# Norm and turn of the tokens for two mixtures moved into the attention ahead of each

## The chip, the cores and the metric

The kernel runs on one core of one Trainium2 chip. The metric is the device time of one execution in microseconds (us). Engines are named as in the profile: PE is TensorE's matmul, PEld its weight load, DVE is VectorE, ACT is ScalarE, POOL is GpSimd, SP is SyncE.

## The reference

The program is four layers over 16 batches of 100 tokens with 256 features. Each layer adds a gated cross attention and then a gated mixture to x. What bears on the change, in short:

```
x = x + tanh(g_xattn[1]) * attention1(layernorm(x), ctx)        # 8 heads of 64
x = x + tanh(g_ffn[1])   * squared_mixture(layernorm(x))
x = x + tanh(g_xattn[2]) * attention2(layernorm(x), ctx)        # 4 heads of 64
x = x + tanh(g_ffn[2])   * linear_mixture(layernorm(x))

squared_mixture(x): shared = square(relu(x @ Ws1)) @ Ws2
                    weight = trunc(softmax(top 2 of x @ Wr))    # 8 experts
                    shared + sum_e weight_e * (square(relu(x @ W1_e)) @ W2_e)
linear_mixture(x):  weight = softmax(top 2 of x @ gate)         # 8 experts
                    sum_e weight_e * (x @ weight_e)
```

The context has 361 rows of 192 features. All of it is float32. A product of two float32 tiles stands in the trace as two records, a transpose as one.

## The kernel before, in words

The program has eight phases on one core: attention 0, a routed mixture, attention 1 (L=1), the squared mixture, attention 2 (L=2), the linear mixture, attention 3, the slot mixture. The order on each engine is the order in which the code is written; engines meet by semaphores. Two phases are parted by `end` and `begin`: each of PE, DVE, ACT and POOL raises `phase_ended` when it has drained, and each waits for all four. Attention 1 follows the routed mixture, and attention 3 the linear mixture, without such a meeting in full.

An attention goes over the batches one at a time (`pipelined`: batches 0, 1, 14 and 15 are written out, the others are a hardware loop of two). While batch t is attended, PE computes the projections of batch t+1 (`step`) and closes batch t-1 (`o_turn`, `project`). Heads come in pairs: four pairs in attention 1, two in attention 2. DVE takes the maxima of the scores (`maximum`, L1440), copies the turned probabilities out of PSUM (`probs_copy`, L1449), which PE needs for `weigh` (L2268), scales the output (`o_scale`, L1456 and L1462), which PE needs for `o_turn` (L2277), and adds the closed batch to X (`residual`, L1470, L1475, and the statistics L1483). `residual(t-1)` stands behind the maxima of heads 2 and 3 and ahead of `probs_copy` of heads 2 and 3.

A mixture of before starts by making its own input from X. `x_stats` (L1631, L1633) reduces the statistics of all 16 batches, POOL raises all 16 columns to the power -0.5 (L827), `pair_norm` (L1639) normalizes one batch, `pair_turn` on PE (L2473) turns two batches into a bank, and `pair_copy` on ACT (L1093) copies them to GXT, the turned tokens that every product of the mixture reads. In the squared mixture PE then computes the logits of all 13 tiles of 128 tokens (`tile_logits`, L2485), and only then the hidden products (`hidden`, L2502: four groups of 400 tokens, nine experts with the shared one) and the products back (`down`, L2518). DVE chooses the experts from the logits (L1648 to L1678) and adds the outputs up (L1815, L1818). In the linear mixture the products are L2547, and the turns stand in three portions among the first logits and the first tile.

For the routed mixture the kernel already does this work inside attention 0: `router_stats` (L1285, L1287), `router_norm` (L1292) and `router_turn` (L2098) handle batch t-1 while later batches are attended.

## Time and profile before

| | us |
|---|---|
| median of 3 runs | 1855.22 (1854.19 to 1857.0) |
| profiled execution, its own time | 1855.15 |
| its span in the trace | 1853.3 |
| PE busy | 1620.0 (87% of the span) |
| PEld busy | 1147.3 (62%) |
| DVE busy | 957.9 (52%) |
| ACT busy | 633.9 (34%) |
| POOL busy | 299.0 (16%) |

The span is what the trace covers; the time of the execution is 1.85 us longer. PE is busy for most of the span, and 70% of the chain that ended last runs over PE. Times below count from the start of the span. Attention 1 ends near 1051 us, attention 2 near 1407 us.

### The profile page before, as it was taken

Reading aid. Unit: us, or ns where it says so; the run is one execution under the profiler, and the core shown is the slowest. Engines: PE = TensorE matmul, PEld = TensorE weight load, DVE = VectorE, ACT = ScalarE, POOL = GpSimd, SP = SyncE. Lnnn points to the kernel's source line nnn. Section 1 sums busy time; section 2 is a strip of 40 time slices with the busy share of each in tenths; the row PEclk is TensorE's granted clock in tenths of the full one; section 3 lists DMA queues with packets and bytes.
Section 4 is the critical chain, followed back from the end, with each engine's and each line's share of the span. In section 5 each row is a group of like instructions: output and inputs, shape, how many; then the busy total and the mean of one; then the engine's idle time right before and its main releaser. Section 6 shows DMA issues by size and latency. Waiting matters only on the chain.

```text
span 1853.3 us, 30331 instructions
## 1 busy us (share of the span) xinstructions
PE 1620.0 (87%) x9090; PEld 1147.3 (62%) x9090; DVE 957.9 (52%) x3011; ACT 633.9 (34%) x1796; POOL 299.0 (16%) x394
## 2 busy tenths in 40 slices
PE   5899899729999999999999799799997998786786
PEld 2555555519999766666666577476775446664554
DVE  4788787422222244444343435545445666765653
ACT  3555455203322233333333233133331014443322
POOL 4545554230000120000000001100000112212000
PEclk9999999859999999999999789899997999997887
DMA  4000006158999410000000000100000101300001
GB/s 106 15 15 15 16 19 199 45 183 287 326 323 331 143 35 13 12 12 12 6 12 7 1 6 18 31 25 18 24 12 1 32 24 42 101 27 1 1 1 36
DMA packets 88418, 117.37 MB, mean 63 GB/s; under 512 B 16428, under 2 KB 80140, under 8 KB 83212
## 3 DMA queue, kind: packets, MB, share of 16 engines
q1 hardware_dynamic: 85228, 113.05, 19.3%
q0 software_dynamic: 2048, 3.29, 0.6%
q8 instruction: 39, 0.64, 0.1%
q14 instruction: 47, 0.39, 0.1%
q10 hardware_dynamic: 1056, 0.01, 0.0%
HBM read 104.51 MB, written 8.52 MB: 61 GB/s over the span
## 4 chain that ended last, share of the span: by engine, by line
PE 70%; issue 12%; DVE 7%; ACT 4%; POOL 3%; DMA 2%; POOLq 0%; DVEq 0%; ACTq 0%; SPq 0%
PE bank L2155 14%; PE bank L2268 7%; PE bank L2446 7%; PE bank L2241 5%; PE bank L2547 5%; PE bank L2214 5%; PE bank L2252 4%; PE bank L2460 3%; PE bank L2298 3%; PE bank L2502 3%; PE bank L2206 3%; PE bank L2518 2%; PE bank L2639 2%; DVE work L1440 1%; ACT work L985 1%
## 5 line engine op out<-in xcount | busy, mean ns | idle before, releaser
L985 ACT ACTIVATE work<-bank,work 100x361 f32<-100x361 f32 (+1 forms) x272 | 158.7, 590 | 251.9 <-DVE work L1440 227.8
L2268 PEld LDWEIGHTS bank<-work 128*100 128x100 f32 x1760 | 183.7, 170 | 58.2 <-issue 29.3
L1449 DVE COPY work<-bank 128x300 f32<-128x300 f32 (+1 forms) x272 | 123.0, 489 | 183.9 <-PE bank L2252 183.4
L2268 PE MATMUL bank<-work 128*100 128x64 f32 (+1 forms) x1760 | 188.0, 258 | 14.2 <-DVE work L1449 14.1
L2446 PE MATMUL bank<-work 128*128 128x128 f32 x1280 | 152.9, 278 | 1.1 <-DMA work<-in_F_b1c 0.6
L2446 PEld LDWEIGHTS bank<-work 128*128 128x128 f32 x1280 | 150.2, 194 | 3.3 <-ACT work L1118 1.2
L1773 DVE SCALAR_TENSOR_TENSOR work<-bank,work 128x128 f32<-128x128 f32 x160 | 56.1, 351 | 180.7 <-PE bank L2446 168.4
L757 POOL TENSOR_TENSOR work<-work,neg_half 100x1 f32<-100x1 f32 x96 | 52.9, 551 | 561.5 <-DVE work L1396 559.8
L1440 DVE TENSOR_REDUCE work<-bank 100x1 f32<-100x361 f32 x208 | 101.9, 528 | 71.8 <-PE bank L2241 60.8
L2241 PE MATMUL bank<-work 64*100 64x361 f32 (+1 forms) x512 | 120.0, 546 | 1.1 <-ACT work L970 0.6
L2252 PE MATMUL bank<-ident,work 100*128 100x100 f32 x880 | 103.0, 251 | 8.6 <-ACT work L985 7.8
L2155 PE MATMUL bank<-L_WkvT,work 96*128 96x512 f32 x192 | 97.9, 634 | 13.4 <-ACT work L946 11.8
L1118 ACT ACTIVATE work<-bank,work 128x128 f32<-128x128 f32 x160 | 58.7, 367 | 144.4 <-PE bank L2446 139.3
L2252 PEld LDWEIGHTS bank<-ident,work 100*128 100x128 f32 x880 | 86.5, 144 | 22.1 <-ACT work L985 12.2
L2547 PE MATMUL bank<-F_weight,work 128*128 128x512 f32 (+1 forms) x208 | 95.1, 617 | 0.0
L2155 PE MATMUL bank<-L_Wv,work 96*128 96x512 f32 x192 | 91.8, 602 | 0.0
L2214 PE MATMUL bank<-work,L_Wk 96*128 96x361 f32 x256 | 90.1, 486 | 0.8 <-DVEq L1353 0.8
L785 POOL TENSOR_TENSOR work<-work,neg_half 128x4 f32<-128x4 f32 x80 | 82.0, 1025 | 12.7 <-DVE work L1422 10.2
L975 ACT COPY work<-bank 128x512 f32<-128x512 f32 (+1 forms) x96 | 45.9, 479 | 101.2 <-PE bank L2155 99.2
L2460 PE MATMUL bank<-work 128*128 128x256 f32 x320 | 72.5, 380 | 0.5 <-DVE work L1773 0.5
L2547 PEld LDWEIGHTS bank<-F_weight,work 128*128 128x128 f32 (+1 forms) x208 | 40.0, 195 | 50.8 <-issue 42.6
L2214 PEld LDWEIGHTS bank<-work,L_Wk 96*128 96x128 f32 x256 | 45.4, 192 | 36.0 <-issue 15.9
(294 smaller groups left out, 2784.0 us busy)
## 6 DMA issues: line engine op xcount, KB each, us to landing
work<-in_F_w SPq DMA_DIRECT2D x60, 1024.0 KB, 5.4
work<-in_ctxT SPq DMA_DIRECT2D x64, 135.4 KB, 2.1
work<-in_ctx SPq DMA_DIRECT2D x32, 192.0 KB, 2.5
sorted_x<-zeros SPq DMA_DIRECT2D x1, 2560.0 KB, 10.4
work<-in_F_b SPq DMA_DIRECT2D x20, 128.0 KB, 5.7
work<-sorted_x SPq DMA_DIRECT2D x20, 128.0 KB, 3.0
sorted_y<-work SPq DMA_DIRECT2D x20, 128.0 KB, 5.4
work<-in_ctx SPq DMA_DIRECT2D x32, 78.8 KB, 2.3
```

The costliest lines, as they stand in the source:

```text
L785: nc.gpsimd.tensor_tensor(rr[j][:, 4 * k:4 * k + 4], rr[j][:, 4 * k:4 * k + 4], neg_half[:, 0:4], ALU.pow).then_inc(s.rqk.sem, 1)
L985: nc.scalar.activation(pr[:, 0:NK], S_bank[k][0:T, 0:NK], ACT.Exp, bias=nmax[k][0:T, :], accum_out=rsum[j][0:T, h:h + 1]).then_inc(s.exped ...
L1440: nc.vector.tensor_reduce(nmax[k][0:T, :], S_bank[k][0:T, 0:NK], axis=AXX, op=ALU.max, negate=True).then_inc(s.maxed.sem, 1)
L1449: nc.vector.tensor_copy(PT[k][:, 0:CH, :], PT_bank[k][:, 0:CH * T].rearrange("p (c t) -> p c t", c=CH)).then_inc(s.probs_copied.sem, 1)
L2155: ins = mm(dst[0:m_out, 0:n_out], lhs(c), w[0:parts[c], c, 0:n_out], start=(c == 0), stop=(c == 1))
L2214: ins = mm(dst[:, 0:NC], wk[L][0:CW[c], c, m * P:(m + 1) * P], CT[j][0:CW[c], c, 0:NC], start=(c == 0), stop=(c == 1))
L2241: ins = nc.tensor.matmul(S_bank[k][0:T, 0:NK], QT[j][b:b + W, m, :], kt(L, j)[b:b + W, m, 0:NK], start=True, stop=True)
L2252: ins = nc.tensor.transpose(PT_bank[k][:, c * T:(c + 1) * T], PR[k][0:T, c, :], ident[0:T, 0:T])
L2268: ins = nc.tensor.matmul(to, PT[k][:, c, :], values, start=(c == 0), stop=(c == CH - 1))
L2446: ins = nc.tensor.matmul(bank[to + f % 2][:, 0:P], W1[j][:, c, col:col + P], TT[j][:, c, :], start=(c == 0), stop=(c == 1))
L2460: ins = nc.tensor.matmul(bank[6 + j][:, 0:D], AC[j][:, f, :], W2[j][:, f, :], start=(f == 0), stop=(f == HID0 // P - 1))
L2547: ins = nc.tensor.matmul(bank[3 + q % Y_BANKS][0:k, :], GXT[:, c, i * P:i * P + k], lin2[:, c, 2 * g:2 * g + 2, :].rearrange("p e n -> p ( ...
```

## The change

Four things change.

1. Inside attentions 1 and 2 each batch is also normalized and turned for the mixture behind. DVE reduces the statistics of batch t right behind them (`mixture_stats`, now from one small tile instead of x_st6), POOL raises one column (`mixture_rstd`), DVE normalizes batch t-1 at the last pair of heads (`mixture_norm`), PE turns batch t-2 into columns 256 to 455 of the bank of the output projection (`mixture_turn`, at the end of `project`), and DVE copies it to GXT (`mixture_keep`, inside `residual`).
2. The heads of both mixtures lose `x_stats`, `pair_norm`, `pair_turn` and `pair_copy`. What is left of batch 15 is done there: its power on POOL, its norm and its copy on DVE, its two transposes on PE.
3. The squared mixture begins with hidden products, and all the logits stand behind the third of them. A group of hidden products waits for the tokens of its own group alone. ACT computes the exponential for the weights behind the ninth product instead of the fourth.
4. GXT lies elsewhere in SBUF, and the four tiles GX become one, GN.

```diff
+            def mixture_rstd(L, t):
+                wait_count(pool, mixture[L].ln_x, 3 * t + 2)
+                nc.gpsimd.tensor_tensor(Rrs[0:T, :], Rrs[0:T, :], neg_half[0:T, 0:1], ALU.pow).then_inc(mixture[L].rstd_x, 1)
...
+                    norms(2, 0)
+                    norms(3, 1)
+                    mixture_rstd(L, 0)
+                    with pool.Fori(1, B // 2 - 1) as i:
+                        for j in range(2):
+                            norms(2 * i + j + 2, j)
+                            mixture_rstd(L, 2 * i + j - 1)
+                    mixture_rstd(L, B - 3)
+                    mixture_rstd(L, B - 2)
...
+            def mixture_stats(L, t):
+                s = mixture[L]
+                wait_for(dve, at[L].x_stats, t + 1)
+                apart(dve)
+                nc.vector.bn_aggr(Rmv[0:T, :], Rst6[0:T, :]).then_inc(s.ln_x, 1)
+                wait_count(dve, s.ln_x, 3 * t + 1)
+                nc.vector.tensor_scalar(Rrs[0:T, :], Rmv[0:T, 1:2], LN_EPS, None, ALU.add).then_inc(s.ln_x, 1)
+            def mixture_norm(L, t):
+                s = mixture[L]
+                wait_count(dve, s.rstd_x, t + 1)
+                nc.vector.tensor_scalar(GN[0:T, :], X[0:T, bass.ds(t, 1), :].rearrange("p o d -> p (o d)"),
+                                        Rmv[0:T, 0:1], Rrs[0:T, :], ALU.subtract, ALU.mult).then_inc(s.ln_x, 1)
+            def mixture_keep(L, t, turned):
+                nc.vector.tensor_copy(GXT[:, :, :].rearrange("p c (b t) -> p c b t", b=B)[:, :, bass.ds(t, 1), :],
+                                      turned[:, TURN_AT:TURN_AT + 2 * T].rearrange("p (c o t) -> p c o t", c=2, o=1)
+                                      ).then_inc(mixture[L].x_copied, 1)
...
                     nc.vector.tensor_tensor(RO[0:T, :], R_bank[0:T, 0:D], bo[L][0:T, :], ALU.add).then_inc(s.resid.sem, 1)
+                    if L in (1, 2) and not (isinstance(t, int) and t == 0):
+                        mixture_keep(L, t - 1, R_bank)
...
+                    if L in (1, 2):
+                        mixture_stats(L, t)
...
+                        if p == PAIRS[L] - 1 and started:
+                            mixture_norm(L, t - 1)
                     o_scale(t, j)
...
-                x_stats(s, 1)
-                for t in range(B):
-                    pair_norm(s, t)
+                dve.wait_ge(s.x_turned, 1)
+                mixture_keep(1, B - 1, bank[6])
...
-                        if g == 0 and c == 3:
+                        if g == 0 and c == E1:
                             exp_difference(s, ROUTE_EXP1, 0, TILES)
...
+            def mixture_turn(L, t, turned):
+                wait_count(pe, mixture[L].ln_x, 3 * (t + 1))
+                for c in range(2):
+                    ins = nc.tensor.transpose(turned[:, TURN_AT + c * T:TURN_AT + (c + 1) * T], GN[0:T, c * P:(c + 1) * P],
+                                              ident[0:T, 0:T])
...
+                    if L in (1, 2) and not (isinstance(t, int) and t == 0):
+                        ins = mixture_turn(L, t - 1, R_bank)
                     ins.then_inc(s.out.sem, 1)
...
-                for u in range(B // 2):
-                    pair_turn(s, u)
-                for i in range(TILES):
-                    tile_logits(s, ew1, i)
                 for g in range(B // 4):
                     for c in range(1 + E1):
                         hidden(g, c)
+                        if g == 0 and c == 0:
+                            mixture_turn(1, B - 1, bank[6]).then_inc(s.x_turned, 1)
+                        if g == 0 and c == 2:
+                            for i in range(TILES):
+                                tile_logits(s, ew1, i)
```

The order of instructions shows it. First PE where attention 1 ends and the squared mixture begins. The lines of the changed file are other ones: L2326 is the output projection (L2298 of before), L2522 the hidden product (L2502), L2505 the logits (L2485), L2133 is `mixture_turn`. Here products of float32 count once. Before:

```order
L2298 MATMUL bank5<-L1_Wo,work 100x256 x4
L2473 MATMUL bank0<-ident,work 128x100 x4
...
L2485 MATMUL bank7<-F1_Wr,work 128x8 x24
L2485 MATMUL bank7<-F1_Wr,work 64x8 x2
L2502 MATMUL bank0<-work,F1_up 128x400 x2
L2502 MATMUL bank1<-work,F1_up 128x400 x2
L2502 MATMUL bank2<-work,F1_up 128x400 x2
```

With the change:

```order
L2326 MATMUL bank5<-L1_Wo,work 100x256 x4
L2133 MATMUL bank5<-ident,work 128x100 x2
L2522 MATMUL bank0<-work,F1_up 128x400 x2
L2133 MATMUL bank6<-ident,work 128x100 x2
L2522 MATMUL bank1<-work,F1_up 128x400 x2
L2522 MATMUL bank2<-work,F1_up 128x400 x2
L2505 MATMUL bank7<-F1_Wr,work 128x8 x24
L2505 MATMUL bank7<-F1_Wr,work 64x8 x2
L2522 MATMUL bank0<-work,F1_up 128x400 x2
```

The 32 transposes ahead of the logits are gone (eight rows of four), two are left behind the first hidden product, and the logits stand behind the third.

Second, PE in the loop of attention 2, around the output projection (L2252 and L2280 turn probabilities, L2241 and L2269 are scores). Before:

```order
L2252 MATMUL bank3<-ident,work 128x100 x3
L168 REGISTER_ALU
L2298 MATMUL bank5<-L2_WoT,work 100x256 x2
L2241 MATMUL bank0<-work 100x361
L2241 MATMUL bank1<-work 100x361
```

With the change:

```order
L2280 MATMUL bank3<-ident,work 128x100 x3
L169 REGISTER_ALU
L2326 MATMUL bank5<-L2_WoT,work 100x256 x2
L181 REGISTER_ALU
L2133 MATMUL bank5<-ident,work 128x100 x2
L2269 MATMUL bank0<-work 100x361
L2269 MATMUL bank1<-work 100x361
```

Two transposes have come in ahead of the scores of heads 2 and 3. Third, DVE in the same loop, from the residual to the scaling of the output (L1501 is L1470 of before, L1508 is L1475, L1516 is L1483, L1480 is L1449, L1487 is L1456). Before:

```order
L1470 TENSOR_TENSOR work<-bank5,L2_bo 100x256
L1475 ISA
L1475 SCALAR_TENSOR_TENSOR X<-work,gates,X 100x256
L168 REGISTER_ALU
L1483 ISA
L1483 BN_STATS x_st6<-X 100x6
L1449 COPY work<-bank2 128x300
L1449 COPY work<-bank3 128x300
L168 REGISTER_ALU
L1456 RECIPROCAL work<-work 100x4
```

With the change:

```order
L1501 TENSOR_TENSOR work<-bank5,L2_bo 100x256
L1348 COPY work<-bank5 128x2x100
L1508 SCALAR_TENSOR_TENSOR X<-work,gates,X 100x256
L1516 BN_STATS work<-X 100x6
L1335 BN_AGGR work<-work 100x2
L1337 TENSOR_SCALAR work<-work 100x1
L1480 COPY work<-bank2 128x300
L1480 COPY work<-bank3 128x300
L1343 TENSOR_SCALAR work<-X,work 100x256
L1487 RECIPROCAL work<-work 100x4
```

The copy to GXT (L1348), the reduction (L1335) and the sum (L1337) have come in ahead of the copies of probabilities, the norm (L1343) ahead of the scaling.

## Rows read from the trace of the kernel before

**Rows 1.** Windows: us, busy PE, PEld, DVE, ACT, POOL, then clock, DMA share, GB/s
```profile
680.00:1049.00 369.00, 356.75 (x2142) 236.82 (x2142) 152.52 (x362) 131.98 (x376) 6.59 (x12) 1.00 0.03 9
...
1190.00:1400.00 210.00, 199.09 (x1257) 147.05 (x1256) 100.02 (x257) 79.72 (x254) 7.68 (x14) 0.99 0.07 19
```

**Rows 2.** Chain that ended last, head of the squared mixture: start, us, what
```profile
1050.62 0.43 DVE x_st L1483
...
1051.49 1.18 DVE work L1631 x16
...
1053.01 2.92 POOL work L827
...
1055.96 0.42 DVE work L1639
...
1056.52 6.15 PE bank L2473 x32
1062.67 10.61 PE bank L2485 x52
1073.28 18.58 PE bank L2502 x48
...
1095.74 4.03 PE bank L2502 x12
```

**Rows 3.** The same chain, head of the linear mixture
```profile
1406.88 0.43 DVE x_st L1483
...
1412.78 1.56 PE bank L2473 x8
1414.34 2.70 PE bank L2485 x12
...
1418.47 8.98 PE bank L2547 x16
...
1429.67 5.10 PE bank L2485 x40
1434.77 78.16 PE bank L2547 x176
```

**Rows 4.** Windows in both heads; the column after POOL is the granted clock
```profile
1062.00:1073.00 11.00, 11.00 (x56) 10.97 (x55) 0.00 (x0) 0.98 (x2) 0.00 (x0) 0.50 0.00 1
1073.00:1078.00 5.00, 5.00 (x11) 2.79 (x11) 4.15 (x54) 0.50 (x1) 0.00 (x0) 0.52 0.01 2
...
1427.00:1434.00 7.00, 6.71 (x54) 5.99 (x52) 5.34 (x13) 1.87 (x4) 0.00 (x0) 0.91 0.01 2
1434.00:1439.00 5.00, 5.00 (x11) 2.50 (x11) 4.46 (x48) 0.41 (x2) 0.00 (x0) 0.50 0.39 100
```

**Rows 5.** Timeline of PE, a pair of transposes and what follows, attentions 1 and 2
```profile
1004.92 0.34 PE L2149 MATMUL bank<-ident,work 100*128 100x100 f32 x2
1005.10 1.40 PE L2214 MATMUL bank<-work,L_Wk 96*128 96x361 f32 x4
...
1302.45 0.39 PE L2149 MATMUL bank<-ident,work 100*128 100x100 f32 x2
1302.67 1.43 PE L2214 MATMUL bank<-work,L_WkT 96*128 96x361 f32 x4
```

**Rows 6.** Timeline, copies of probabilities behind the residual, and PE's weighing behind the last
```profile
990.80 0.85 DVE L1449 COPY work<-bank 128x300 f32<-128x300 f32 x2 [1.37 <-PE bank L2252]
...
1311.53 0.85 DVE L1449 COPY work<-bank 128x300 f32<-128x300 f32 x2 [1.02 <-PE bank L2252]
1313.34 1.19 PE L2268 MATMUL bank<-work 128*100 128x64 f32 x12
```

**Rows 7.** Timeline of DVE in attention 0, the same reduction of one batch
```profile
303.16 0.18 DVE L1285 BATCH_NORM_AGGREGATE work<-work 100x2 f32<-100x6 f32 x1
```

**Rows 8.** Timeline of PE, last batch of attention 2, waiting for DVE
```profile
1400.76 1.27 PE L2268 MATMUL bank<-work 128*100 128x64 f32 x12 [0.49 <-DVE work L1449]
```

**Rows 9.** Timeline of DVE, first output of the squared mixture that is added up
```profile
1092.83 0.48 DVE L1815 TENSOR_SCALAR work<-bank,gates 128x256 f32<-128x256 f32 x1 [9.23 <-PE bank L2518]
```

More of the change, by code:

```diff
@@ L59 @@
 ROUTER_AT, LOGITS_AT = 256, 456
+TURN_AT = 256
 BATCHES_BACK = ((0, 2), (2, 6), (6, 11), (11, B))
@@ L427, in flamingo_kernel @@
         Fmv, Frs = area.take(B, 2), area.take(B)
+        area.at = attention_end
+        GXT, GN = area.take(2, NTOK), area.take(D)
+        assert area.at <= attention_end + B * D
         area.at = unused_by_3
-        GX = [area.take(D) for _ in range(4)]
-        GXT = area.take(2, NTOK)
         GLG, GV8, GI8 = area.take(TILES, 8), area.take(TILES, 8), area.take(TILES, 8, dt=U32)
@@ L815, in attention @@
                     three_deep(pool, attend, lambda t, j: None)
-                else:
+                elif L == 3:
                     with pool.Fori(0, B // 2 - 1) as i:
@@ L819, in attention @@
                             norms(2 * i + j + 2, j)
+                else:
+                    norms(2, 0)
[7 more added lines that the diff above has]
+                    mixture_rstd(L, B - 2)
                 end(pool)
@@ L855, in squared_experts @@
             def squared_experts():
-                rstd_x(mx1, 3, last=False)
+                begin(pool, 3)
+                mixture_rstd(1, B - 1)
                 add_rows(mx1)
             def linear_experts(while_adding):
-                rstd_x(mx2, 5, last=False)
+                begin(pool, 5)
+                mixture_rstd(2, B - 1)
                 add_rows(mx2, while_adding)
@@ L1156, in linear_experts @@
                 begin(act, 5)
-                for u in range(B // 2):
-                    pair_copy(s, u)
-                    if u == 1:
-                        exp_difference(s, ROUTE_EXP2[0], 0, FIRST_TILES)
+                exp_difference(s, ROUTE_EXP2[0], 0, FIRST_TILES)
                 exp_difference(s, ROUTE_EXP2[1], FIRST_TILES, TILES)
@@ L1785, in squared_experts @@
                 nc.vector.memset(GLG[:, TILES - 1, :], 0.0).then_inc(s.route, 1)
+                mixture_norm(1, B - 1)
                 dve.wait_ge(loaded[3], 16 * n_loads[3])
@@ L1788, in squared_experts @@
                 dve.wait_ge(s.route, 1)
-                x_stats(s, 1)
-                for t in range(B):
-                    pair_norm(s, t)
+                dve.wait_ge(s.x_turned, 1)
+                mixture_keep(1, B - 1, bank[6])
                 n = choose(s, 1, 0, TILES)
@@ L1828, in linear_experts @@
                 dve.wait_ge(s.route, 1)
-                x_stats(s, 2)
-                for t in range(8):
-                    pair_norm(s, t)
+                mixture_norm(2, B - 1)
                 def route(n, k, lo, hi):
@@ L1851, in linear_experts @@
                 n = route(1, 1, 0, FIRST_TILES)
-                for t in range(8, B):
-                    pair_norm(s, t)
+                dve.wait_ge(s.x_turned, 1)
+                mixture_keep(2, B - 1, bank[0])
                 for i in range(TILES):
@@ L2465, in routed_experts, with kept @@
                 end(pe)
-            def pair_turn(s, u):
-                wait_count(pe, s.x_copied, u - 1)
-                for m in range(2):
-                    pe.wait_ge(s.ln_x, B + 1 + 2 * u + m + 1)
-                    for c in range(2):
-                        ins = nc.tensor.transpose(bank[u % 2][:, (2 * m + c) * T:(2 * m + c + 1) * T],
-                                                  GX[(2 * u + m) % 4][0:T, c * P:(c + 1) * P], ident[0:T, 0:T])
-                ins.then_inc(s.x_turned, 1)
-            def turned(i):
-                return -(-(i * P + tile_rows(i)) // (2 * T))
+            def kept(tokens):
+                return -(-tokens // T)
             def tile_logits(s, w, i):
-                pe.wait_ge(s.x_copied, turned(i))
                 k = tile_rows(i)
+                pe.wait_ge(s.x_copied, kept(i * P + k))
                 for c in range(2):
@@ L2519, in down @@
                                          down1[:, c, :], start=True, stop=True).then_inc(s.out, 1)
-                for u in range(B // 2):
-                    pair_turn(s, u)
-                for i in range(TILES):
-                    tile_logits(s, ew1, i)
                 tiles = 0
@@ L2550, in experts @@
                     ins.then_inc(s.out, 1)
-                for u in range(2):
-                    pair_turn(s, u)
                 for i in range(FIRST_TILES):
                     tile_logits(s, ew2, i)
-                for u in range(2, 4):
-                    pair_turn(s, u)
+                mixture_turn(2, B - 1, bank[0]).then_inc(s.x_turned, 1)
                 for g in range(4):
                     experts(0, g)
-                for u in range(4, B // 2):
-                    pair_turn(s, u)
                 pe.wait_ge(s.route, 1 + FIRST_TILES)
```

23 lines of the change are left out of this document (5 added, 18 removed).

## The prediction

> **What bounds the kernel now.** I read the page first: PE is busy 87% of the span and carries most of the chain that ended last, so what matters is where PE computes and where it waits. Then I cut the span into stages. Inside attentions 1 and 2 PE is busy 357 of 369 us and 199 of 210 us at a granted clock of 1.00 and 0.99, with DVE at 41% and 48% [rows 1]: anything added to PE there costs its time in full, and DVE has room as long as what it adds is not ahead of something PE waits for. The heads of the two mixtures are different. In the squared one the chain leaves attention 1 on DVE at 1051.05 (1050.62 + 0.43), goes over the reduction of 16 statistics, POOL's power (2.92 us) and one norm, and reaches PE at 1056.52; PE then turns for 6.15 us and computes logits for 10.61 us, and the first product of the mixture proper starts at 1073.28 [rows 2]. That is 22.2 us from the end of the attention to the first hidden product, all of it on the chain. In the linear one the attention ends at 1407.31, PE starts at 1412.78, and the long run of products that ends the phase starts at 1434.77, 27.5 us later [rows 3].
>
> The clock matters in both heads. PE is busy without a gap through the logits of the squared mixture and still has 0.50 of full speed, which is the 1.2 GHz level, and it stays at 0.52 in the first 5 us of hidden products [rows 4]. The first 48 records of hidden products take 18.58 us where 12 at full speed take 4.03 [rows 2], so the slow start costs 18.58 - 4 x 4.03 = 2.46 us. In the linear mixture the clock is at full speed when 40 records of logits start (5.10 us, 0.1275 each, against 10.61 / 52 = 0.204 in the other head), and the products behind them run at 0.50 again [rows 3, 4].
>
> **The change part by part.**
>
> *Pairs of transposes in the attentions.* Batch t-2 is turned in the `project` of batch t-1, so batches 2 to 15 of each attention carry one pair: 28 pairs. A pair of the same shape followed directly by other work moves PE on by 0.18 us (1004.92 to 1005.10) and by 0.22 us (1302.45 to 1302.67) [rows 5]. I take 0.20: 28 x 0.20 = 5.6 us lost. Bounds: nothing less than 0.17 seems open, since PE is the bound; at the half clock a pair is 2 x 6.15 / 32 = 0.38 [rows 2], which makes 10.8 us.
>
> *DVE inside the residual.* The copy of 128x200 out of PSUM is smaller than the 128x300 copies (0.85 us for two) [rows 6]; I take 0.40. The reduction is 0.18 in attention 0 [rows 7]; with the sum of one column, which I put at as much, and their waits I take 0.45 together. So about 0.85 us (up to 1.1 with the loop's register work) comes in ahead of the copies of probabilities. There DVE waits 1.37 us for PE in attention 1 and 1.02 us in attention 2 [rows 6]. In attention 1 that covers it; in attention 2 it covers it just, and a copy that starts 0.1 us late is still over long before PE's weighing at 1313.34, since both copies are done at 1312.38 [rows 6]. So I cost it at nothing in the loops. If the cover were gone, what is late is `weigh` of heads 2 and 3, then `o_scale`, then PE's `o_turn`. In the last batch of each attention there is no projection of a next batch to hide it: in attention 2 PE already waits 0.49 us there for exactly this copy [rows 8]. So 0.85 us is paid once per attention: 1.7 us.
>
> *Norm and power.* `mixture_norm` (0.42 us, the row of L1639 [rows 2]) comes in ahead of `o_scale`, where DVE waits for PE's last weighing; POOL has 7 and 8 us of work in the two stretches [rows 1], and the norm stands two copies behind the sum that POOL waits for, which is about the time of one power. Nothing, covered by PE's weighing; without that cover o_scale and the first maxima would be late by up to 0.4 us a batch.
>
> *Ends of the attentions.* Behind the last projection stand a pair of transposes at the half clock (0.38), the copy (0.40) and reduction and sum (0.45): the attentions end 1.2 us later. I allow 0.3 us for PE to leave the meeting.
>
> *Head of the squared mixture.* Hidden products can start at 1051.05 + 1.2 + 0.3 = 1052.55 instead of 1073.28, 20.7 us sooner. Given back behind the start: the pair of batch 15 (0.38), the logits, 52 records now behind hidden products and so at full speed (52 x 0.1275 = 6.6), and a second slow start, because in the other head the clock was down behind logits (2.46). The gain is 20.7 - 9.4 = 11.3 us. Is anything late? The pair of batch 15 waits for POOL's power and a norm, about 1.2 us, while the first hidden product covers 2.7 us (four records, 0.67 each at half speed). DVE needs the weights before the first output: logits end near 1066, the exponential now comes behind the ninth product near 1077, and the weights, a few short operations later, are ready near 1079, while the first output is there near 1081. DVE waits 9.23 us for it now [rows 9], about 2 us then.
>
> *Head of the linear mixture.* From the end of attention 2 of before: 1.2 + 0.3, 12 records of logits (2.70), the pair (0.38), the first tile with its slow start (8.98) and 40 records of logits (5.10) make 18.7 us against 27.5 [rows 3]. The gain is 8.8 us. The route on DVE is ready sooner by as much as the logits are, so it stays behind them as before.
>
> The sum, against the profiled execution's own 1855.15 (0.07 under the median of the runs): 1855.15 - 11.3 - 8.8 + 5.6 + 1.7 = **1842.35 us**.
>
> *A rule weighed against the rows.* PE at 0.50 through 16.7 us of transposes and logits without a gap, then at full speed some 5 us into the hidden products [rows 2, 4]: the kind of work decides here. The Trainium skill, "TensorE: Matmul & The Clock Gate", Part 1 (the HAM clock gate), says that activity opens the gate and idling closes it; its Part 4 (PE-mode transpose) says that transposes don't count as busy in the same way. By Part 1 alone the logits of before would already run at full speed, and moving them would gain 10.61 - 6.6 = 4.0 us less, 1846.4 us; the trace does not agree with that.
>
> **The rivals.**
>
> *The clock stays up behind the logits.* Both heads then save a slow start of about 2.5 us: 1842.35 - 2.46 - 2.5 = 1837.4. For it: in the changed head only hidden products come first, and PE never idles. Against it: behind 40 such records it was at 0.50 [rows 4], and now there are 52. This is what the skill's Part 1 rule, that the gate closes when PE idles, would give.
>
> *The logits fall to the half clock on the way.* 52 records x 0.204 instead of 6.6: 4.0 us more, 1846.4. For it: in the window of the 40 records the clock was at 0.91, so it fell toward the end [rows 4]. A part of this is likely.
>
> *DVE becomes what PE waits for in the attentions.* The place is `probs_copy` of heads 2 and 3 behind the longer residual. If its 0.85 us showed in every one of 28 batches, the time would be 1842.35 + 28 x 0.85 = 1866, slower. It decides from (1855.15 - 1842.35) / 28 = 0.46 us a batch on. Against it stand the waits of 1.02 and 1.37 us and the slack behind them [rows 6]. A part of it, 0.2 to 0.4 us a batch, gives 1848 to 1853.5.
>
> *The heads don't shorten,* since hidden products wait for something else that is as late as before: 1855 or a little over, with the price in the attentions still paid, up to 1862. Against it: the weights were loaded long ago (the DMA share is 0.00 in the logits' window [rows 4]), and the first group needs four batches alone.
>
> **How the numbers follow.** The forecast, with its own range of 1839.5 to 1845.5 (pairs of 0.17 to 0.22, a slow start more or less, some logits at half speed): 0.60. Clock stays up: 0.13. Logits at half speed: 0.11. Part of the DVE delay: 0.07. DVE in full: 0.05. Heads don't shorten: 0.04. The range of 8 in 10 reaches over the two clock cases, 1836.5 to 1849. A measurement of this kernel tells 0.2%, 3.7 us, from no change. Up to 1851.5 it counts as faster, which holds all of the first three cases and more than half of the partial delay; the rest of that and half of the last case lie within, the others behind. Faster by more: 0.88; within: 0.05; slower: 0.07.
>
> **What would show it.** In the changed profile hidden products start some 1.5 us behind the end of attention 1 at a clock of 0.50 for about 5 us; logits take 6.6 us at full speed and what follows is at half; PE's share in the attentions stays at 95 to 97% with no new wait for the copies of probabilities in the loops; a period of a batch grows by 0.2 us; DVE waits about 2 us for the first output. It would be wrong with a wait of PE for L1449's counterpart in every batch, or if the period grew by over 0.4 us.

## The result, and where the time went

The changed kernel takes 1836.78 us (median of 4 runs, 1835.95 to 1841.66) against 1856.11 us (4 runs) for the kernel before: ratio 0.9897, 95% interval 0.9881 to 0.9913. Forecast were 1842.35 us and a range of 1836.5 to 1849. So 19.3 us were won where 12.8 were forecast. The profiled execution took 1835.95 us with a span of 1834.1. In a later comparison six more executions of the changed kernel had a median of 1841.33 us against 1855.97, ratio 0.992 (0.9901 to 0.9939): 14.6 us.

To compare executions I cut each span at the same events, read from the timelines of PE and DVE: the first product of an attention, the end of the statistics of its last residual, the first record of the squared mixture's `down`, the first product of the linear mixture's long run, and the first scores of attention 3. All in us:

| stretch | before | after | after, once more | forecast change |
|---|---|---|---|---|
| start to attention 1 | 632.82 | 631.03 | 636.89 | 0 |
| attention 1 to its last statistics | 418.23 | 421.50 | 421.60 | +4.4 |
| to first `down` (head, squared mixture) | 40.65 | 27.15 | 27.05 | -12.05 |
| to attention 2 | 96.54 | 96.58 | 96.46 | 0 |
| attention 2 to its last statistics | 219.07 | 222.54 | 222.57 | +4.4 |
| to the long run (head, linear mixture) | 27.39 | 17.02 | 17.05 | -9.55 with the next |
| to attention 3 | 89.16 | 88.43 | 87.34 | |
| to the end | 329.44 | 329.85 | 330.94 | 0 |

The last column is the change that the forecast's terms give for each stretch. The cuts lie at the last statistics, so the reduction and sum behind them (0.45 us each) count in the heads. The two attentions cost 6.7 us together instead of 8.8. The heads with the long run give 24.6 us instead of 21.6. And 1.8 us came from a stretch that the change does not touch; it is 4.1 us the other way in a second execution of the same kernel, so it is no gain. From attention 1 to the end the changed kernel takes 1203.1 and 1203.0 us, the one before 1220.5. I take 17.4 us as what the change is worth, between the 19.3 and 14.6 of the medians.

The kernel before has one profile alone, and the cut doesn't take out all the scatter. In the experiment with the order alone, whose attention 1 has the code of before, that attention took 422.10 us instead of 418.23: its first batch, to PE's turn of the scaled output (`o_turn`), took 48.06 us instead of 44.70, with a second stretch at the half clock from 663.8 to 670.6 us. What repeats is the period of a batch in the loops: in all executions with the same loop code its mean agrees within 0.02 us.

The windows of both attentions in the changed kernel (us, busy PE, PEld, DVE, ACT, POOL, clock, DMA share, GB/s) answer [rows 1]:

```profile
680.00:1045.00 365.00, 353.93 (x2141) 236.62 (x2140) 163.60 (x418) 131.62 (x374) 14.87 (x27) 1.00 0.03 9
1195.00:1393.00 198.00, 186.99 (x1217) 140.62 (x1216) 109.15 (x307) 73.46 (x235) 15.41 (x28) 1.00 0.07 19
```

PE is as busy as before (97% and 94%), and DVE has gone from 41% to 45% and from 48% to 55%. In attention 2 the timelines of PE and of DVE show what the pair of transposes does on PE, and how short DVE's wait for the probabilities has become, 0.60 us where it was 1.02 [rows 6]:

```profile
1295.07 1.03 PE L2326 MATMUL bank<-L_WoT,work 128*100 128x256 f32 x4
1295.94 0.34 PE L2133 MATMUL bank<-ident,work 100*128 100x100 f32 x2
1296.20 0.85 PE L2269 MATMUL bank<-work 64*100 64x361 f32 x4
...
1391.77 1.27 PE L2296 MATMUL bank<-work 128*100 128x64 f32 x12 [1.13 <-DVE work L1480]
```

```profile
1298.31 0.36 DVE L1348 COPY work<-bank 128x200 f32 x1
...
1300.66 0.85 DVE L1480 COPY work<-bank 128x300 f32<-128x300 f32 x2 [0.60 <-PE bank L2280]
```

From projection to scores PE takes 1.13 us (1295.07 to 1296.20), where the kernel before took 0.96 (1321.45 to 1322.41). The period of a batch grows by the same: from one batch's `o_turn` to the next it goes in the mean from 25.16 to 25.33 us in attention 1 and from 13.12 to 13.29 in attention 2. In the loops PE never waits for L1480; the 1.13 us above is the last batch, where it was 0.49 [rows 8].

The chain that ended last, from the last projection of attention 1 to the second tile, answers [rows 2]:

```profile
1050.54 0.35 PE bank L2133 x2
1050.89 0.02 issue
1050.91 0.42 DVE work L1501
1051.34 0.27 DVE work L1348
1051.61 0.40 DVE X L1508
...
1052.10 0.44 DVE work L1516
...
1052.63 0.19 DVE work L1335
...
1052.85 0.15 DVE work L1337
...
1053.11 3.04 PE bank L2522 x4
1056.15 0.33 PE bank L2133 x2
1056.48 3.88 PE bank L2522 x8
1060.37 5.78 PE bank L2505 x52
1066.15 13.70 PE bank L2522 x36
1079.85 3.88 PE bank L2538 x18
```

Between the last statistics and the first hidden product lie only 0.57 us, where POOL's power, a norm, 32 transposes and 52 logits lay before. The same chain in the linear mixture answers [rows 3]:

```profile
1399.38 2.73 PE bank L2505 x12
1402.11 0.43 PE bank L2133 x2
1402.53 9.11 PE bank L2568 x16
1411.64 4.25 PE bank L2505 x40
1415.89 77.43 PE bank L2568 x176
```

And the clock in the squared mixture's head (the column behind POOL), to be read beside [rows 4]:

```profile
1053.00:1058.00 5.00, 4.89 (x9) 2.80 (x10) 0.85 (x4) 0.50 (x1) 0.55 (x1) 0.50 0.00 0
...
1060.00:1066.00 6.00, 6.00 (x54) 5.83 (x52) 0.00 (x0) 0.93 (x2) 0.00 (x0) 0.96 0.01 3
1066.00:1069.00 3.00, 3.00 (x7) 1.66 (x7) 2.75 (x37) 0.00 (x0) 0.00 (x0) 0.51 0.00 0
1069.00:1074.00 5.00, 5.00 (x17) 2.79 (x16) 1.41 (x19) 3.62 (x8) 0.00 (x0) 1.00 0.01 2
```

The hidden products start at the 1.2 GHz level, the logits run nearly whole at 2.4 GHz, then the clock is down for 3 us of hidden products although PE never paused (6.00 of 6.00 and 3.00 of 3.00 us busy). DVE waits 2.51 us for the first output, forecast 2. It waits for PE's product and not for its own weights, so the weights are not late:

```profile
1080.82 0.48 DVE L1837 TENSOR_SCALAR work<-bank,gates 128x256 f32<-128x256 f32 x1 [2.51 <-PE bank L2538]
```

### The profile page after: what moved, and what is told of

The parts are those of the page before. It is cut to its first block, busy times and chain, and to the rows that moved or that the text cites. A ratio compares the mean times of both kernels' runs of the same rounds, so it can differ in the third digit from the quotient of the medians.

```text
span 1834.1 us, 30494 instructions
## 1 busy us (share of the span) xinstructions
PE 1615.2 (88%) x9090; PEld 1146.1 (62%) x9090; DVE 970.7 (53%) x3073; ACT 627.5 (34%) x1780; POOL 311.0 (17%) x424
## 4 chain that ended last, share of the span: by engine, by line
PE 70%; issue 12%; DVE 7%; ACT 4%; POOL 3%; DMA 2%; POOLq 0%; DVEq 0%; ACTq 0%; SPq 0%
PE bank L2183 14%; PE bank L2296 7%; PE bank L2476 7%; PE bank L2568 5%; PE bank L2269 5%; PE bank L2242 5%; PE bank L2280 4%; PE bank L2490 3%; PE bank L2326 3%; PE bank L2522 3%; PE bank L2234 3%; PE bank L2538 2%; PE bank L2655 2%; DVE work L1471 1%; ACT work L1005 1%
## 5 line engine op out<-in xcount | busy, mean ns | idle before, releaser
L1480 DVE COPY work<-bank 128x300 f32<-128x300 f32 (+1 forms) x272 | 123.0, 489 | 172.0 <-PE bank L2280 171.5
L2269 PE MATMUL bank<-work 64*100 64x361 f32 (+1 forms) x512 | 119.6, 544 | 1.1 <-ACT work L990 0.6
L2280 PE MATMUL bank<-ident,work 100*128 100x100 f32 x880 | 103.4, 252 | 8.9 <-ACT work L1005 8.1
L2183 PE MATMUL bank<-L_WkvT,work 96*128 96x512 f32 x192 | 96.3, 625 | 13.5 <-ACT work L966 11.8
L2280 PEld LDWEIGHTS bank<-ident,work 100*128 100x128 f32 x880 | 87.1, 145 | 22.3 <-ACT work L1005 12.4
```

The costliest lines, as they stand in the source:

```text
L1480: nc.vector.tensor_copy(PT[k][:, 0:CH, :], PT_bank[k][:, 0:CH * T].rearrange("p (c t) -> p c t", c=CH)).then_inc(s.probs_copied.sem, 1)
L2183: ins = mm(dst[0:m_out, 0:n_out], lhs(c), w[0:parts[c], c, 0:n_out], start=(c == 0), stop=(c == 1))
L2269: ins = nc.tensor.matmul(S_bank[k][0:T, 0:NK], QT[j][b:b + W, m, :], kt(L, j)[b:b + W, m, 0:NK], start=True, stop=True)
L2280: ins = nc.tensor.transpose(PT_bank[k][:, c * T:(c + 1) * T], PR[k][0:T, c, :], ident[0:T, 0:T])
```

## The experiments

All ratios are to the kernel before, with 95% intervals. Medians of the kernel before lay between 1855.8 and 1856.4 in the comparisons, but the stretch ahead of attention 1 differs by up to 8 us between executions, so the readings rest on the stretches defined above, of one execution each.

The expected times, but for the order alone in the kernel before, were worked out from the changed kernel's 1836.8 us. The measured medians all came out above the expected times, mostly by 2 to 7 us. A part of this is the starting value, since the changed kernel itself came out at 1841.33 when it was repeated.

### Each pair of transposes twice

```diff
+                        mixture_turn(L, t - 1, R_bank)
                         ins = mixture_turn(L, t - 1, R_bank)
```

> The changed kernel, with the pair of transposes done twice in every output projection of attentions 1 and 2 (same source, same place). Theory: PE is the bound there and pays 0.17 us a pair at full speed, 0.35 at the two ends: 28 x 0.17 + 2 x 0.35 = 5.5 us over the changed kernel's 1836.8, so 1842.3, and the period of a batch grows from 25.33 to 25.50 and from 13.29 to 13.47. Rival: the pair fills time in which PE would wait anyway, and the growth seen in the changed kernel came from DVE's longer residual: then under 1.5 us more.

Measured: 1848.21 us, ratio 0.9954 (0.9937 to 0.9971); expected were 1842.3. The profiled execution was the shortest of the nine, 1843.22 us. In it the periods grow again by 0.17 us, to 25.51 and 13.46 (from 25.33 and 13.29), attention 1 takes 424.62 us (+3.1) and attention 2 takes 224.47 (+1.9), 5.0 us together. That is the theory's price; the other 5 us between this execution and the median have no profile. PE is the bound in both loops, and a pair costs 0.17 us there.

### Logits ahead of the hidden products, as before

```diff
+                mixture_turn(1, B - 1, bank[6]).then_inc(s.x_turned, 1)
+                for i in range(TILES):
+                    tile_logits(s, ew1, i)
...
                 for g in range(B // 4):
...
-                        if g == 0 and c == 0:
-                            mixture_turn(1, B - 1, bank[6]).then_inc(s.x_turned, 1)
-                        if g == 0 and c == 2:
...
```

> The changed kernel, but the squared mixture turns batch 15 and computes all its logits ahead of the first hidden product, as before the change. Theory: the logits run at 1.2 GHz (10.6 us instead of 5.8, 4.8 more), there is one slow start of 2.5 us instead of two of 2.9 and 1.6 (2.0 less), and PE waits for POOL's power, norm and copy of batch 15 (1.7 more): 1836.8 + 4.5 = 1841.3. Rival, by which busy PE opens the clock whatever it computes: the logits reach full speed on their way, under 2 us more, 1838.5 at most.

Measured: 1846.01 us, ratio 0.9934 (0.9915 to 0.9952); expected were 1841.3. The chain:

```profile
1058.95 10.25 PE bank L2505 x52
1069.20 18.16 PE bank L2522 x48
```

and the clock:

```profile
1058.80:1069.20 10.40, 10.40 (x55) 10.35 (x53) 0.37 (x1) 0.00 (x0) 0.00 (x0) 0.52 0.01 2
```

PE is busy for all of 10.40 us and the clock stays at 0.52. The logits don't open it, which is against the rival; the head takes 30.37 us, 3.2 more than with the logits inside, where the theory had 4.5.

### The order of the logits alone, in the kernel before

The logits go behind the third hidden product, and the exponential behind the ninth, as in the changed kernel:

```diff
-                        if g == 0 and c == 3:
+                        if g == 0 and c == E1:
                             exp_difference(s, ROUTE_EXP1, 0, TILES)
...
-                for i in range(TILES):
-                    tile_logits(s, ew1, i)
...
+                        if g == 0 and c == 2:
+                            for i in range(TILES):
+                                tile_logits(s, ew1, i)
```

> The kernel before, with norm, turn and copies at the head as they were, and only the order changed in the squared mixture: all logits behind the third hidden product, the exponential behind the ninth. Theory: logits at full speed (4.8 less), slow starts 2.9 and 1.6 instead of 2.5 (2.0 more): 2.8 us less than before, 1853.3. Rival: the order is most of the gain of the squared mixture's head, 8 us or more, under 1848.

Measured: 1855.65 us, ratio 0.9995 (0.9974 to 1.0016): no difference in the whole time is shown. The head takes 38.94 us, 1.7 less than before, where the theory had 2.8 and the rival 8 or more; the logits took 6.72 and the 36 hidden records behind them 14.38. Both are more than in the changed kernel (5.78 and 13.70). So the order was worth 1.7 us of the 13.5 that the head gained; the rest comes from norm, power and transposes, which left it.

### The squared mixture alone

The test for both mixtures is cut to the squared one, and the linear one gets its norm and turn in pairs of batches back:

```diff
...
-                    if L in (1, 2) and not (isinstance(t, int) and t == 0):
+                    if L == 1 and not (isinstance(t, int) and t == 0):
...
```

> The change for attention 1 and the squared mixture alone; attention 2 and the linear mixture as before. Theory, from the stretches of the two traces: attention 1 pays 3.75 us, the head gains 13.9, so 10.2 less than before, 1845.9. Rival: the two halves depend on each other (over the clock or over what is loaded when), and the gain is off by more than 2 us from that.

Measured: 1848.19 us, ratio 0.995 (0.9927 to 0.9972). Expected were 1845.9, with more than 2 us off as the sign of the rival, and it is 2.3 off. In the profiled execution the head of the linear mixture takes 27.38 us (27.39 before) and attention 2 takes 217.36, 1.7 less than the 219.07 before; its loop has the period of before, and the difference lies in its first batch and its end. Attention 1 takes 423.10 us (421.50 in the changed kernel) and the squared mixture's head 28.69 (27.15). From attention 1 to the end it is 1211.3 us, 9.2 less than before where 10.2 were expected. So each half has its gain without the other, within the 1 to 2 us by which these stretches scatter; a smaller dependence is not excluded.

### The logits in four portions

```diff
-                        if g == 0 and c == 2:
-                            for i in range(TILES):
+                        if g == 0 and 2 <= c <= 5:
+                            for i in range((0, 4, 7, 10)[c - 2], (4, 7, 10, 13)[c - 2]):
```

> The changed kernel, but the 13 tiles of logits of the squared mixture stand in portions of 4, 3, 3 and 3 behind the third to the sixth hidden product instead of in one block. Theory: the second fall of the clock in that head comes from the block of logits; between portions PE computes hidden products, so the clock stays at 1.00 and the 1.6 us of the second slow start are saved: 1835.2, and from the end of attention 1 to the first product back 25.5 us instead of 27.2. Rival: the clock falls for small products however they are spread, or falls on its own at that time: no difference, 27 us, 1836.8.

Measured: 1835.37 us, ratio 0.9896 (0.9871 to 0.9921). The head takes 22.78 us instead of 27.15, and 25.5 were expected:

```profile
1055.97 2.71 PE bank L2522 x8
1058.68 1.68 PE bank L2505 x16
1060.37 1.45 PE bank L2522 x4
1061.81 1.24 PE bank L2505 x12
...
1068.30 8.26 PE bank L2522 x24
```

The clock does not fall again. The head gained more than one fall, since there was no slow start either: the clock was back at 1.00 at 1052.6 us, ahead of the first hidden product, and the first 12 hidden records took 4.3 us instead of 6.9. So I repeated it.

### The same portions once more, and the changed kernel once more

> The logits of the squared mixture in four portions once more. Theory (a solid block of logits lets the clock fall, portions between hidden products do not): the stretch to the first down product is again near 23 us and no half clock stands behind the logits. Rival (the clock's fall depends on the phase of each execution): a second stretch at half clock appears here too, and the stretch is 25 us or more. Time by the theory about 4 us under the changed kernel, 1832 to 1834; by the rival 1834 to 1837.

> The changed kernel once more, unchanged, beside the others of this call: about 1836.8 us, ratio 0.990 to the kernel before. What it adds is how much the stretch from the last statistics of attention 1 to the first down product (27.15 us) and the clock in it repeat from one execution to the next.

Measured on one chip: portions 1840.22 us, ratio 0.9903 (0.9884 to 0.9922); the changed kernel 1841.33 us, ratio 0.992 (0.9901 to 0.9939). Expected were 1832 to 1834 and 1836.8. The heads take 24.47 and 27.05 us. Windows, portions first:

```profile
1061.00:1067.00 6.00, 5.96 (x14) 3.31 (x15) 0.85 (x3) 1.43 (x3) 0.55 (x1) 0.72 0.00 0
1067.00:1077.00 10.00, 10.00 (x66) 8.12 (x65) 0.12 (x2) 3.71 (x8) 0.00 (x0) 1.00 0.01 2
```

```profile
1066.00:1072.00 6.00, 6.00 (x54) 5.87 (x52) 0.00 (x0) 0.93 (x2) 0.00 (x0) 0.95 0.01 3
1072.00:1075.00 3.00, 3.00 (x6) 1.68 (x6) 2.85 (x38) 0.01 (x1) 0.00 (x0) 0.54 0.00 0
```

The slow start differs from one execution to the next (the head is 1.7 us longer than in the first run of portions); the second fall does not. In the squared mixture's head every profiled execution with the solid block of 52 behind hidden products, nine in all with the other experiments, begins it at full clock and has a fall 3.5 to 5.3 us behind the block's start, and none of the three with portions has one. I had expected nearly 23 us for the repeat and bounded the rival at 25; 24.47 lies between, and the windows decide it for the theory.

In the whole time the portions are not shown to be faster: the intervals overlap. From attention 1 to the end they take 1199.5 and 1201.6 us against 1203.1 and 1203.0. A part of the head's gain is missing there: the linear mixture's head took 18.8 us in both instead of 17.0, and only about 1.2 us of that came back behind it.

### The solid block three chunks later

```diff
-                        if g == 0 and c == 2:
+                        if g == 0 and c == 5:
```

> The same solid block of 52 logits, put behind the sixth hidden chunk instead of the third. If the block itself lets the clock fall, the fall comes again, some 6 us after the block's start, with hidden products at half clock behind it, and the stretch to the first down product stays near 27 us, or a little more if the routing now comes late. If it was the place (soon after the slow start that follows attention 1), the clock stays at full speed and the stretch falls to about 24 to 25 us.

Measured: 1842.64 us, ratio 0.9916 (0.9899 to 0.9933); the head takes 27.59 us.

```profile
1069.40:1073.00 3.60, 3.60 (x35) 3.60 (x33) 0.00 (x0) 0.93 (x2) 0.00 (x0) 0.98 0.02 5
1073.00:1077.00 4.00, 4.00 (x21) 3.95 (x22) 0.13 (x2) 0.00 (x0) 0.00 (x0) 0.50 0.00 0
1077.00:1080.00 3.00, 3.00 (x6) 1.53 (x7) 2.93 (x41) 0.17 (x1) 0.00 (x0) 0.56 0.00 0
```

The clock falls inside the block, 3.5 us behind its start, and the block takes 7.38 us. It is the block, not its place behind the slow start.

### In the last batch, the residual behind the copies of probabilities

In the last batch of attentions 1 and 2 nothing of the residual is left ahead of the copies of probabilities. The addition to X and the copy to GXT go directly behind the last of them, statistics and norm behind the scaling of the output:

```diff
-                        if p == 0 and started:
+                        if p == 0 and started and more:
                             residual(t - 1, 1 - j)
...
-                            mixture_norm(L, t - 1)
+                            if more:
+                                mixture_norm(L, t - 1)
+                            else:
+                                residual_add(t - 1, 1 - j)
                     o_scale(t, j)
+                    if PAIRS[L] and not more:
+                        residual_stats(t - 1, 1 - j)
+                        mixture_norm(L, t - 1)
```

> The changed kernel, but in the last batch of attentions 1 and 2 the addition to X and the copy to GXT stand behind the last copies of probabilities, and statistics and norm of batch 14 behind the scaling of the output. Theory: in the last batch DVE's residual is ahead of copies that PE waits for; moved, it saves 0.8 us in attention 1 (last batch 16.4 to 15.6) and 0.9 us in attention 2 (9.65 to 8.8): 1835.1. Rival: what is moved only comes ahead of the scaling and the last turn instead, and nothing is saved.

Measured: 1838.71 us, ratio 0.9911 (0.9884 to 0.9937); expected were 1835.1, and in the whole time no gain is shown. The last batch shrinks from 16.39 to 15.92 us and from 9.65 to 8.63. Attention 2 is 1.0 us shorter (221.58); attention 1 only 0.2 (421.31), since its last projection ran longer at the half clock (3.43 us instead of 2.93). The term of the forecast for the last batches is real, and 0.5 and 1.0 us of it can be had back.

### Three more copies of the turned tokens per batch

The copy to GXT is made four times, which puts 1.4 us more into DVE's residual of each batch (1.76 us for four, 0.36 for one).

```diff
+                for k in range(3 + 1):
...
```

> The changed kernel, with every copy to GXT done four times, each behind the one before (about 0.5 us each, 1.5 us more in every residual). Theory: in the loop of attention 2 DVE has 0.60 us of waiting and 1.35 us between its first copy and PE's weighing, 1.95 us in all, more in attention 1: the periods stay at 25.33 and 13.29, and only the last batches and the two ends pay, 4 x 1.5 = 6 us: 1843. Rival (DVE becomes what PE waits for): the periods grow by up to 1.5 us, up to 42 us more, 1879.

Measured: 1849.9 us, ratio 0.9966 (0.9948 to 0.9984); expected were 1843. The periods don't move (25.33 and 13.30), but the last batches grow by 4.7 and 1.8 us, where I had 1.5 each. In attention 1's last batch PE waits 1.75 us for L1484 (L1480 of the changed kernel) at 1041.66, and then:

```profile
1040.00:1048.00 8.00, 6.34 (x32) 5.06 (x33) 4.53 (x12) 2.22 (x8) 0.55 (x1) 0.55 0.00 0
1048.00:1056.00 8.00, 6.33 (x30) 5.12 (x30) 2.15 (x5) 0.66 (x3) 0.00 (x0) 0.50 0.00 0
```

In the changed kernel the first of these windows stands at 1.00. So in the loops DVE has at least 1.4 us more to give, and in this last batch, which waited 1.4 us longer for the copies (1.75 instead of 0.34) and grew by 4.7, the clock's fall cost more than the wait.

### Eight more copies

The same edit with `range(8 + 1)`: nine copies instead of one.

> The same with nine copies instead of one, 4 us more in every residual. Theory: past the cover of 1.95 us attention 2 pays the rest, about 2.0 us a batch (period 13.3 to 15.3), attention 1 at most 0.5 us a batch, and last batches and ends 16 us: about 1836.8 + 27 + 6 + 16 = 1886. Rival: if the cover were larger than read, the periods stay and the time is near 1853; if it were smaller, attention 1 pays too and the time is above 1900.

Measured: 1905.91 us, ratio 1.0251 (1.022 to 1.0282). Attention 1's periods grow by only 0.18 us with 3.8 us more of DVE work (4.12 us in one piece). Attention 2 takes 278.86 us, 56.3 more:

```profile
680.00:1045.00 365.00, 352.00 (x2106) 234.31 (x2106) 197.94 (x517) 128.09 (x367) 14.32 (x26) 1.00 0.03 9
1195.00:1460.00 265.00, 233.72 (x1289) 171.05 (x1288) 153.84 (x430) 80.75 (x254) 15.96 (x29) 0.86 0.05 15
```

I had expected about 2 us a batch, 1886 us in all. In attention 2 a batch of the loop takes 16.8 us in the mean instead of 13.3, 3.5 more. Over the whole attention, first product to last statistics, PE's waits for L1484 add up to 26.2 us and its idle time grows by 23.0 us, but its busy time grows by 33.3 us (207.68 to 241.02) for 1309 records instead of 1308, with the clock at 0.84 instead of 0.98. The only batch of the loop with no time at half clock took 15.09 us, 1.8 more, which is what the theory had; the others took 15.3 to 17.9. That is the rival in which DVE is what PE waits for, as it would look.

### Portions and late residual together

Both edits as they stand above.

> Both edits that helped, together: logits of the squared mixture in four portions, and in the last batch of attentions 1 and 2 only the addition of the residual stands ahead of the copies of probabilities, the statistics and the norm behind them. The two act in different stretches, so the sum of their parts: 27.15 down to about 23 us in the head, 0.2 and 1.0 us in the attentions' ends, about 1831.5 us, ratio about 0.987. If the clock's phase takes the gain of the portions back, about 1835.

Measured: 1835.82 us, ratio 0.9885 (0.9866 to 0.9904), the lowest ratio of all, against 1831.5 us and 0.987 expected; in the same comparison the changed kernel had 0.992. The intervals overlap. By stretches: head 22.79 us (27.05), attention 2 221.44 (222.57), head of the linear mixture 16.05 (17.05). Attention 1 took 2.9 us more (424.54). Its first batch is at fault: 47.96 us to its `o_turn` against 44.71, in code that this kernel shares with the late residual alone, which took 44.70; there is a second stretch at the half clock from 668.6 to 675.4 us, as in the order alone. From attention 1 to the end: 1198.7 us against 1203.0.

## Why the prediction was right, and what was mis-sized

**The parts and their places** held. What left the two heads left the path, what entered the loops of the attentions cost PE's time and nothing else, and both sides were sized well enough for the range of 8 in 10. Not by much: 1836.78 lies 0.3 us inside its lower bound and outside of 1839.5 to 1845.5, the range of the forecast's own mechanism. The bound stood there for the rival in which the clock stays up in both heads, which did not happen in that profile. The later median of 1841.33 lies inside both ranges, so a part of the distance is scatter, and that the first measurement still fell into the range is partly luck. The forecast missed 6.4 us of gain in the profiled execution: 1.3 of that is not the change (the stretch ahead of attention 1 gave 1.8, the last one and the one ahead of attention 2 took 0.45), 2.1 lies in the attentions and 3.0 in the heads.

**Pairs of transposes**: 0.17 us each, at the lower bound of the forecast's 0.17 to 0.22; doubling them confirmed it. 28 pairs cost 4.8 us, not 5.6. The rows that I had read it from were pairs followed by loads for another product; the step from the start of the projection to the scores, with and without the pair, gives it directly.

**DVE's residual in the loops** cost nothing, as forecast. DVE waits 0.60 us for the probabilities where it waited 1.02, and the three extra copies show at least 1.4 us more of cover in both attentions. In attention 1 even 3.8 us more of DVE work made the period only 0.18 us longer. My "covers it just" looked at DVE's wait alone; the slack behind it, which the forecast named, was the larger part. With it the rival "DVE becomes what PE waits for" falls. But its price counted the wait alone. With eight copies 3.8 us more of DVE work, of which at least 1.4 were covered, cost 3.5 us a batch in attention 2, and 33.3 of the 56.3 us in all were longer busy time, through the clock.

**Last batches and ends**: forecast 0.85 us and 1.2 us per attention. The last batch grew by 0.71 and 0.81 us with its pair in it, so DVE's part is 0.54 and 0.64. The end of attention 1 grew by some 0.8 us: 0.35 for the pair, but 0.27 on the chain for the copy (0.36 long; the next operation starts under it) and 0.19 + 0.15 for reduction and sum, with 0.2 made up by the last projection (2.93 us, 3.14 before). The end of attention 2 grew by 0.95. PE left the meeting in 0.1 us, not 0.3.

**Logits at full speed**: 5.78 us for 52 (0.111 each) and 4.25 for 40 (0.106), where I had 6.6 and 5.10. This is the term that failed most, 1.7 us of the 3.0. The row of 0.1275 each came from a stretch whose clock was 0.91 [rows 3, 4], so it held a part at half speed, and I used it as the price at full speed. I had seen that clock, and gave it to a rival instead of correcting for it. The window of 7 us held other work too; cut to the block's own 5.10 us it reads

```profile
1429.67:1434.77 5.10, 5.10 (x41) 5.05 (x40) 4.17 (x11) 0.49 (x1) 0.00 (x0) 0.81 0.02 5
```

and 5.10 x 0.81 = 4.1 us, close to the 4.25 measured.

**The second slow start**: 36 hidden records took 13.70 us; at 0.336 each they would take 12.1, so it cost 1.6 us and not 2.46. The first one cost more than forecast: twelve records and the pair took 7.25 us, 6.87 were forecast. In the linear mixture the long run took 77.43 us, 0.73 less than before.

**The clock rivals.** "The clock stays up" did not happen in the changed kernel's squared mixture: 0.51 at 1066 to 1069 us with PE busy 3.00 of 3.00, and so in all nine executions with a solid block of 52 behind hidden products. In the linear mixture, with its block of 40, it did happen in the repeat of the changed kernel and in the run with the logits first: there is no fall behind the block, and in the repeat the stretch behind it took 87.34 us instead of 88.43. The twelve other executions have a fall inside that block or up to 1.3 us behind it. So for the shorter block the rival was open. It gave nothing in the whole: the 1.1 us were lost again in the last stretch (330.94 us instead of 329.85). In the repeat:

```profile
1413.00:1430.00 17.00, 16.66 (x69) 9.63 (x68) 11.46 (x67) 0.41 (x2) 0.76 (x1) 1.00 0.15 41
```

The Trainium skill, "TensorE: Matmul & The Clock Gate", Part 1, says that idling closes the gate; here it closed without idling. "Logits fall to half clock on the way" happened only in the last 0.6 us of the block in the first profile and in the repeat. In the seven other executions with that block the clock fell 0.7 to 4 us ahead of its end (the block took 7.38 us three chunks later), and so it did inside the linear mixture's block in seven of fourteen, four of them with the changed linear mixture. The forecast's time of the first rival, 1837.4, is nearest to the measured one; by its mechanism it was still wrong. That time came from smaller prices, not from a clock that stayed up, and portions show what the latter gives in the squared mixture's head: 2.6 us, and 4.4 where the slow start was missing too.

**What stays open**: why the first slow start differs (4.3 or 5.9 us for the first twelve hidden records with portions), why the squared mixture alone had 1.5 us more in its head than the changed kernel, and why the logits of the order alone took 6.72 us. The two levels of the clock explain their sizes; what sets the moment of a change was not tried, nor what it is in a block of 8-column products that brings the clock down. The new place of GXT in SBUF was not tried alone; the periods leave nothing to it in the loops, since the pair accounts for all of their 0.17 us.

## What to carry to other kernels

Small work on TensorE that stands alone between phases (transposes, products of a few columns) cost twice here: by itself, and by the half clock that it kept or brought. Spread it over a loop that is already at full speed, in portions between wide products. Take a duration from a row only together with the clock of its own window, and correct for it before you use it elsewhere. Before a busy engine's idle time is spent as cover, look at the batch in which that cover is missing (the last), and count what a wait of TensorE does to the clock as well as the wait.

## What the runs showed of the hardware that I had not expected

The clock fell 3.5 to 5.3 us behind the start of a solid block of logits (52 records of 8 columns) in all nine executions in which it stood behind hidden products, with PE busy all the time, and was back at 1.00 after 2.8 to 6.1 us of hidden products. The same 52 records in portions of 12 and 16 between hidden products ran at 1.00 throughout in the three executions tried. With the block of 40 such records in the linear mixture a fall came, inside it or up to 1.3 us behind it, in twelve of fourteen executions.

In a wait of 1.75 us in the last batch of attention 1 the clock fell and stayed at half for 17 us (1040.9 to 1057.9, the run with three more copies). PE was busy 79% of the window from 1040 to 1048; in the same window of the changed kernel it was busy 77%, at 1.00. That the wait brought the fall is likely, but only one such batch was looked at; with eight more copies one batch with a wait of 1.64 us in attention 2 stayed at 1.00.

The same 40 logits of the linear mixture took 4.25 us in some executions and 5.77 in others, in kernels that do not differ in that mixture; the clock stood at 1.00 and, here with portions, at 0.70:

```profile
1408.70:1414.50 5.80, 5.80 (x42) 5.75 (x40) 2.31 (x8) 0.00 (x0) 0.00 (x0) 0.70 0.24 57
```

And two executions of the changed kernel differ by 5.9 us before attention 1 begins, part of it in the first 80 us, where the clock stood at 1.00 in the first profile and here (the repeat) at:

```profile
0.00:40.00 40.00, 21.59 (x44) 10.00 (x45) 20.71 (x81) 10.73 (x28) 15.74 (x27) 0.92 0.53 122
40.00:80.00 40.00, 35.35 (x165) 19.90 (x164) 25.11 (x88) 21.93 (x61) 18.82 (x26) 0.95 0.04 9
```

Such scatter is a third of this change's gain; a cut at events inside the program takes this part of it out.
